# A two-layer decoder on one core: query and key turning split, a new order of work, a router with a narrow moving operand

## What is computed

```python
x = ln(x + L0_attn(x))            # 32 heads, low-rank queries and keys, rope, causal
x = ln(x + L0_xattn(ctx_512, x))  # adjacency: top 30% of q.k, mixed with x
x = ln(x + L0_ffn(x))             # 7 experts, 2 chosen per token, and a shared one
x = ln(x + L1_attn(x))            # 16 heads of 16 features, rope, causal
x = ln(x + L1_xattn(x, ctx_512))  # softmax over a normalised bilinear form
x = ln(x + L1_ffn(x))             # silu(x.Wg) * (x.Wu), then Wd; hidden size 1024
```

```python
q = rms_norm(x @ q_a_w, q_a_ln_w) @ q_b_w      # 192 low-rank features, 32 x (128 + 64)
ckv = x @ kv_a_w                               # 64 shared latent features, 64 rotated
k_rot = apply_rope(ckv[..., 64:])
gate = xt @ Wr + br                            # the router: 256 features to 7 experts
_, ids = jax.lax.top_k(gate + gate_bias, 2)
```

## Time and profile before

| | us |
|---|---|
| median of three runs | 673.74 (673.16 to 674.34) |
| profiled execution, own time | 674.2 |
| its span in the trace | 672.3 |
| TensorE busy | 651.7 (97%) |
| VectorE busy | 524.2 (78%) |
| ScalarE busy | 502.5 (75%) |
| GpSimd busy | 389.5 (58%) |
| TensorE's granted clock over the span | 0.997 |

### The profile page before, as it was taken

One profiled execution on the slowest core, in us unless ns is written; L12 is line 12 of the kernel. 1 busy time (PEld: TensorE's weight loads), 2 busy tenths in 40 slices (PEclk: granted clock), 3 DMA queues, 4 the chain that ended last, 5 costly groups with the idle time before them and its releaser, 6 DMA issues.

```text
span 672.3 us, 15731 instructions
## 1 busy us (share of the span) xinstructions
PE 651.7 (97%) x5342; PEld 557.9 (83%) x5342; DVE 524.2 (78%) x1684; ACT 502.5 (75%) x1305; POOL 389.5 (58%) x646
## 2 busy tenths in 40 slices
PE   8899999999999999999999999999989999999996
PEld 5589988989888899889877888889878887778885
DVE  2799988996999799767889945557798878858455
ACT  4799778878688885898887866665658786876544
POOL 3388658457664845698769455545872321445543
PEclk9999999999999999999999999999999999999998
DMA  8763022214213211310032012111020000011201
GB/s 259 188 186 86 18 71 59 77 26 118 49 56 103 49 50 47 95 33 2 1 96 63 1 54 87 48 49 47 1 95 5 3 3 4 3 48 48 94 1 63
DMA packets 35048, 40.17 MB, mean 60 GB/s; under 512 B 7052, under 2 KB 27798, under 8 KB 34968
## 3 DMA queue, kind: packets, MB, share of 16 engines
q1 hardware_dynamic: 34424, 38.84, 19.8%
q10 hardware_dynamic: 544, 0.33, 0.2%
HBM read 29.05 MB, written 1.05 MB: 45 GB/s over the span
## 4 chain that ended last, share of the span: by engine, by line
PE 82%; DVE 7%; ACT 4%; SPq 2%; issue 2%; DMA 1%; POOL 1%; DVEq 0%; POOLq 0%; ACTq 0%
PE bank L1242 72%; PE bank L1256 8%; SPq L2762 1%; PE bank L1542 1%; ACT probs L1922 1%; DMA xT_plain<-in_xT 1%; POOL qT L2487 1%; DVE bn L2034 1%; DMA qT<-xT_plain 1%; DVE ctx_pair_lo L2011 1%; DVE y L2011 1%; DVE probs L2162 1%; DVE g_pair_lo L2011 0%; ACT x L1684 0%; ACT xT_hi L1677 0%
## 5 line engine op out<-in xcount | busy, mean ns | idle before, releaser
L2484 POOL TENSOR_SCALAR probs<-probs,soft 128x256 f32<-128x256 f32 (+1 forms) x256 | 104.9, 432 | 52.1 <-DVE soft L2170 51.0
L1784 ACT ACTIVATE probs<-probs,soft 128x256 f32<-128x256 f32 (+1 forms) x256 | 113.2, 448 | 12.0 <-DVE soft L2162 11.1
L2487 POOL TENSOR_TENSOR w_split_lo<-w_raw,w_split_hi 128x512 fp32r<-128x512 f32 (+2 forms) x57 | 74.3, 1311 | 67.9 <-ACT w_split_hi L1677 67.7
L1242 PE MATMUL bank<-xT_hi,w_split_hi 128*128 128x512 f32 x256 | 103.8, 405 | 3.7 <-DVE xT_lo L2014 2.5
L1242 PE MATMUL bank<-xT_lo,w_split_hi 128*128 128x512 f32 x256 | 100.5, 393 | 0.0
L1242 PE MATMUL bank<-keyT,qT 128*64 128x192 f32 (+3 forms) x1024 | 80.4, 302 | 1.3 <-POOL qT L2487 1.3
L1242 PEld LDWEIGHTS bank<-keyT,qT 128*64 128x64 f32 x1024 | 74.2, 137 | 8.9 <-issue 3.6
L1242 PE MATMUL bank<-xT_hi,w_split_lo 128*128 128x512 f32 x192 | 75.5, 393 | 0.0
L2487 POOL TENSOR_TENSOR qT<-qT,xT_plain 64x512 f32<-64x512 f32 x44 | 56.5, 1283 | 31.8 <-DMA qT<-xT_plain 29.7
L2162 DVE CUSTOM_DVE_ANT_0 probs<-bank,mask 128x128 f32<-128x128 f32 (+1 forms) x192 | 58.0, 330 | 17.2 <-PE bank L1242 16.2
L1677 ACT ACTIVATE probsT<-bank 128x384 f32<-128x384 f32 x128 | 53.6, 494 | 13.9 <-PE bank L1256 13.4
(11 more groups left out here) (259 smaller groups left out, 1820.6 us busy)
## 6 DMA issues: line engine op xcount, KB each, us to landing
qT<-xT_plain SPq DMA_DIRECT2D x88, 64.0 KB, 2.0
w_raw_heads<-in_w_o SPq DMA_DIRECT2D x8, 512.0 KB, 4.6
w_raw<-in_w_nopeT SPq DMA_DIRECT2D x8, 384.0 KB, 3.1
qT<-rope_buf SPq DMA_DIRECT2D x40, 64.0 KB, 2.0
w_raw<-in_w_gateT SPq DMA_DIRECT2D x8, 256.0 KB, 2.7
w_raw<-in_w_upT SPq DMA_DIRECT2D x8, 256.0 KB, 3.1
w_raw<-in_w_downT SPq DMA_DIRECT2D x8, 256.0 KB, 3.6
w_raw<-in_L_ffn_Wup SPq DMA_DIRECT2D x7, 256.0 KB, 2.6
```

Source lines behind the costliest of these rows:

```text
L1242: return t.matmul(out, lhsT, rhs, start=start, stop=stop, skip_group_check=shared)
L1784: ins = s.activation(p[:, at], p[:, at], ACT.Exp, bias=st[:, 0, r:r + 1], scale=-1.0, accum_out=st[:, 1, r:r + 1])
L2484: return g_.tensor_scalar(out, in0, s1, s2, op0, op1)
L2487: return g_.tensor_tensor(out, in0, in1, op)
```

## The change

The edits, beside the names and lines that follow from them.

1. **Keys apart.** `down_T h` keeps the eight query blocks; the four key blocks become `key_T h`, with its own signal `keyT_copied`. On VectorE the keys' scaling is its own step `key_scale`.
2. **Early root table.** ScalarE runs a dummy Sqrt (into `last_root`) behind its two load issues at the start.
3. **First loads.** `xT0`, `xT1`, then the weights of groups 0 and 1, then `xT2`.
4. **Two early query buffers.** `q 0 0 0` needs `down_T 0` alone, `q 0 0 1` also `key_T 0`; the first gets a buffer of its own (`qT_first`), both have fixed places.
5. **Router.** The tokens (`xT_hi`, `xT_lo`, 128x128) are stationary and 14 columns move: the seven of `w_router` as fp32r and the seven of its rest (`w_router_parts`, made by two VectorE instructions in the constants' step). Sixteen matmuls a half as before, each now on the whole array; the copy and the transposition are gone, VectorE adds the two parts.
6. **The end.** `f_end` is cut: `f_mid 0` (batch 2, blocks 4 to 6), `f_mid 2` (batch 3, tile 1, blocks 4 to 6), `f_end 0` (batch 2, block 7), `f_mid 1` (tile 0, blocks 4 to 6), `f_end 1` (both tiles, block 7).
7. **Last store** of eight is issued by ScalarE's queue. In `out1` the bias matmuls of both tiles come first.
8. **Order.** A new `PE_ORDER` (523 steps), a new `ASIDE`, new costs, and a cost of leaving each grouping of the array (`LEAVE`) in place of one `MODE`.

```diff
 PE_ORDER = steps_of("""
-down 0, w_k 0, down 1, w_q 0, down_T 0, w_v 1, w_k 1, q 0 0 0, down_T 1, w_q 1, adj_w, w_v 0, adj_qk, q 0 0 1,
-q 1 0 0, s 0 0 0, s 1 0 0, q 1 0 1, adj_sim 0, s 0 0 1, ...
+down 0, down 1, down_T 0, w_k 0, key_T 0, w_q 0, adj_w, w_k 1, w_v 0, w_v 1, key_T 1, down_T 1, adj_qk, q 0 0 0,
+q 0 0 1, adj_sim 0, q 1 0 0, w_q 1, w_k 2, s 0 0 0, q 1 0 1, s 1 0 0, s 0 0 1, ...
...
-f_up 1 7, f_end 0, f_end 1""")
+f_up 1 7, f_mid 0, f_mid 2, f_end 0, f_mid 1, f_end 1""")
...
-    ("adj_mask", 2, 1): 193, ("att_mix", 3): -60, ("down_root", 1): -24, ...
+    ("adj_mask", 2, 1): 58, ("adj_top", 1, 8): 146, ("down_root", 1): 5, ...
...
-    HOP, TABLE, MODE = 0.2, 1.3, 0.13
+    HOP, TABLE = 0.2, 1.3
+    LEAVE = {"": 0.09, "cols64": 0.13, "cols32": 0.135, "rows64": 0.085, "quarter": 0.13}
...
-LOADS_AFTER = [("xT0", "xT1"), ("xT1", "xT2")] + [("xT2", name) for name in (
+LOADS_AFTER = [("xT0", "xT1"), ("xT1", 0), ("xT1", "xT2")] + [("xT2", name) for name in (
...
-FIRST_Q = ("q", 0, 0, 0)
+EVERY_TURNED = [(name, h) for h in range(NHALF) for name in ("down_T", "key_T")]
+TURNED_FOR = {("q", 0, 0, 0): [("down_T", 0)], ("q", 0, 0, 1): [("down_T", 0), ("key_T", 0)]}
+MID_TILES = [[(0, j) for j in range(TB)], *[[(1, j)] for j in range(TB)]]
+LAST_STORED = (B - 1, TB - 1)
+EARLY_PLACE = {("q", 0, 0, 0): (0,), ("q", 0, 0, 1): (1,)}
...
+            elif name == "key_T":
+                h, = k
+                w.wait_ge(*landed("identity"))
                 w.wait_ge(*key_rot[h])
                 out = wait_bank(("keyT", h))
                 for i, tile in enumerate(tiles_of[h]):
                     w.wait_ge(*key_lat[tile])
                     ins = transpose(out[:, i * P:(i + 1) * P], key_tok[:, tile, :])
-                ins.then_inc(lowT_ready.sem, 1)
+                ins.then_inc(keyT_ready.sem, 1)
...
             elif name == "route_lin":
...
-                terms = [(c, plain(part)) for c in range(DC) for part in (xT_pair.hi, xT_pair.lo)]
-                for n, (c, xt) in enumerate(terms):
-                    for i, tile in enumerate(tiles_of[h]):
-                        ins = mm(out[32 * i:32 * i + NE, 0:P], w_router[:, c, :], xt[:, c, tile * P:(tile + 1) * P],
-                                 n == 0, n == len(terms) - 1, True)
+                terms = [(part, c) for c in range(DC) for part in (xT_pair.hi, xT_pair.lo)]
+                for i, tile in enumerate(tiles_of[h]):
+                    for n, (part, c) in enumerate(terms):
+                        ins = mm(out[:, i * 2 * NE:(i + 1) * 2 * NE], part[:, c, tile * P:(tile + 1) * P],
+                                 w_router_parts[:, c, :, :], i == 0 and n == 0, n == len(terms) - 1, True)
                 ins.then_inc(route_ready.sem, 1)
-            elif name == "route_gate":
-                h, = k
-                w.wait_ge(*route_copied[h,])
-                transpose(wait_bank(step)[:, 0:P], gate_T[h][:, :]).then_inc(route_ready.sem, 1)
...
                 for i in range(TB):
+                    mm(out[:, i * D:(i + 1) * D], ones1[:, :], bias1[:, 3 * D:], i == 0, False, True)
+                for i in range(TB):
                     part = out[:, i * D:(i + 1) * D]
-                    mm(part, ones1[:, :], bias1[:, 3 * D:], i == 0, False, True)
...
+                    w.wait_ge(*zeroed["unit"])
+                    s.activation(last_root[:, 0:1], plain(ones1[:, 0:1]), ACT.Sqrt)
...
+        b, i = LAST_STORED
+        w.wait_ge(*last_normed[b, i])
+        s.dma_start(out_dram[b, i * P:(i + 1) * P, :], x[:, TB * b + i, :]).then_inc(stored[b], 16)
...
+                    own(v.tensor_copy(w_router_parts[:, :, 0, :], w_router[:, :, :]))
                     w.wait_ge(*own.now)
+                    own(tt(w_router_parts[:, :, 1, :], w_router[:, :, :], plain(w_router_parts[:, :, 0, :]), ALU.subtract))
```

253 lines of the change are left out of this document (134 added, 119 removed), and 4 rows, old and new, of the table ASIDE.

## The result

| | before | after |
|---|---|---|
| time, median of 11 executions, same chip | 674.22 us (673.16 to 675.29) | 678.15 us (675.67 to 681.76) |
| profiled execution, span | 674.2, 672.3 | 678.62, 676.7 |
| mean granted clock | 0.997 in the profiled execution; 0.992 to 0.999 in the executions of the comparisons below | 0.984 to 0.996 in the 11 |

The ratio is 1.0053, with a 95% interval of 1.0036 to 1.0071. The change makes the kernel slower by some 4 us; the prediction was 672.3, in a range of 669.0 to 675.3. Within the 11 executions of after the time goes with the clock: 675.67 at 0.996, 678.15 at 0.991, 681.76 at 0.984.

A forecast was written before the change was run, and what follows sets the result against it. TensorE, busy 651.7 of 672.3 us, was taken as the bound. The terms -1.5 + 1.3 - 0.1 + 0.4 - 1.4 = -1.3 gave 672.9 for an execution like the profiled one; forecast median 672.3, range 669.0 to 675.3.

The forecast's parts named there:

- start, to the first scores: From the start to the first scores: -1.5 us, from -1.85 + 0.3; ends -2.7 and -0.3.
- switches: TensorE's switches between array groupings: 13 more at 0.10 each, +1.3 us; ends +0.8 and +1.7.
- router's own work: Router on TensorE: 32 matmuls at 0.085, 2.7 us against 2.8 before, -0.1; ends +0.6 and -1.9.
- waits in the middle: TensorE's waits between start and end: half of the 2.8 us left would go, -1.4; ends -2.8 and +2.
- end: After the cut of `f_end`: VectorE starts 0.6 later, last store gives -0.25; +0.4 us, ends 0 and +0.7.
- the 2.50 wait is filled: Start, before `q 0 0 0`: `adj_w` and six other steps placed ahead fill TensorE's 2.50 us wait for turned queries.
- first scores after 38: Start: a sign that the prediction would be wrong, if the first scores came after 38 us.
- The chain is 1.28 shorter: Start: the root table's load leaves half 0's chain, 1.28 us shorter, `xT_lo` near 20.3 rather than 23.09.
- Rival E: Router: the load's duration sets the pace, +0.6 rather than -0.1, 673.0 us; part of the forecast's range, no separate chance.
- D: Attention: `pv` waits for `probsT` in 8 places where `pT` and `pv` stand close; +4, about 676.5 us; chance 0.18.
- B: Start gives nothing: `xT2` lands near 14 rather than 12.5, the 1.5 go; 673.7 to 674 us; chance 0.22.
- no wait over 0.5 before `q 0 0 0`: Start: sign expected in the profile after, TensorE waiting nowhere over 0.5 us before the first query step.

The follow-up runs named there:

- run 12: Also before_root_only: kernel before, with one early dummy square root on ScalarE so that its table loads at the start; 674.73 us, ratio 0.9996.
- before_router_early: Kernel before, with the second half's old router directly behind TensorE's wait for the turned tokens; 674.0 us, ratio 0.9992.
- run 8: Also after_warm_wait: changed kernel, with twelve unread products of 512 columns in `adj_w` before its wait; 675.82 us, ratio 1.0028.
- run 5: Kernel before, with the new router's narrow products directly behind the wait for the turned tokens; 677.44 us, ratio 1.0046.
- Run 6: Changed kernel, with the router's 16 columns moved eight times over (128 moving columns); 678.98 us, ratio 1.0074.
- runs 1 and 3: Changed kernel. 1: second half's router behind the first expert's first pass, 683.66 us; 3: also `adj_w` behind the weights' steps of groups 0 and 1, 685.09 us.
- after_ww_rows_later: Changed kernel, with 128-column router, twelve products in `adj_w`'s wait and GpSimd's clearing of second-layer rows behind `e_u 4 1`; 675.27 us, ratio 1.0004.
- after_tuned: Changed kernel, with 128-column router, `adj_w` later, group 2's loads behind the first queries' swap, `w_k 2` behind the first scores, other engines replanned; 683.0 us.
- after_wide_and_warm: Changed kernel, with 128-column router and twelve products in `adj_w`'s wait, GpSimd's clearing not moved; 677.74 us, ratio 1.0031.
- runs 13 and 6: 13: changed kernel, twelve products in `adj_w`'s wait, second half's router moved behind `e_u 0 1` on TensorE alone, 679.15 us; 6: see Run 6.
- run 7: The run after_ww_rows_later: changed kernel, 128-column router, `adj_w`'s wait filled, GpSimd's clearing moved behind `e_u 4 1`; 675.27 us, ratio 1.0004.

## Why the prediction was wrong

Time by term, from the profiled executions:

| term | forecast | measured |
|---|---|---|
| start, to the first scores | -1.5 | +1.0, with 1.7 of clock in it |
| switches | +1.3 | 9 x 0.1 fit the +1.0 of the first attention; not measured one by one |
| router's own work | -0.1 | +0.75 |
| clock behind the router | not foreseen | +3.4 |
| waits in the middle | -1.4 | idle time: -0.15 in the first attention, -0.2 in the experts, -0.76 in the second layer |
| end | +0.4 | +0.6 |

**The start: the step that failed** is "the 2.50 wait is filled". I listed `adj_w` among the steps that fill it and did not ask what `adj_w` itself waits for: I worked out SP's queue for `xT2` and not for this load, issued at 17.45. That is 2.93 us where the term had none, with some 1.7 of clock behind it. The prediction's own sign of being wrong, first scores after 38, is what came (39.13). What I had looked at came out: 1.50 for `xT2` (I said 1.2), `xT2`'s issue at 7.16 (6.6). "The chain is 1.28 shorter" was wrong by itself too, as run 12 shows: the table was not on the chain alone. `xT_lo` did come early, at 18.67, more than that term allows; the table alone gives none of it. In after's trace the three weight splits stand behind `xT_lo` and the first half's keys are scaled by 15.7, so VectorE's order is what differs; no run here tried that alone.

**The clock: a mechanism that was on no list.** I read in the earlier trace rows a granted clock of 1.00 in all stretches and took it for a constant. In the profiled execution of before it was one. It isn't in each: in before_root_only and before_router_early, with the same start, it fell behind the wait of 2.5 us. The change puts the router's narrow products behind a wait, where the clock fell each time, and a longer wait in the start, where it fell in two of three profiled executions; neither my terms nor my rivals priced this. The runs say how much: filling the start's wait gives back 2.3 us (run 8), the narrow form alone costs 3.4 (run 5), of which 0.75 is its pace (both against runs of other comparisons). These do not add up to the 3.9 of the medians, as the clock differs from execution to execution, and each run carries other small waits.

**The router: the right mechanism, the wrong end of it.** I put its pace between 0.028 and 0.107 and chose 0.085, by the turnings of the earlier trace rows. It was 0.111: 32 x 0.111 = 3.55 against 2.8 before, +0.75. The 0.83 ns a column from the earlier trace rows, which I made the upper end, was the pace. The Trainium skill, "TensorE: Matmul & The Clock Gate", section on LDWEIGHTS, has a load of P columns take P/1.2 ns, 107 ns for 128 by estimate, and the pace in the trace agrees within 4 ns. Run 6 shows the same pace for 16 and for 128 moving columns. Rival E had it right. In the experts' +3.07, 3.4 of clock and 0.75 make 4.15; waits are 0.2 less, and some 0.9 that remain I cannot place.

**Switches and waits in the middle.** Nine switches more by 0.10 are +0.9, and the first attention lost 0.96 while TensorE's idle time went from 2.03 to 1.88. So the switch term fits, and the wait term did not hold for this part: the 1.01 at 227.56 is gone, and this has come,

```profile
120.16 0.65 PE L1251 MATMUL bank<-keyT,qT_first 128*64 128x192 f32 x4 [1.08 <-POOL qT_first L2509]
```

a wait for the same kind of operand. In the second layer idle time went from 4.27 to 3.51, -0.76, of which `kT`, 0.78 before and 0.23 now, is the largest part. The other 0.45 of the -1.2 is less busy time, where four switches more should have added 0.4; I cannot place it. In sum the waits gave 1.1 of my 1.4, near in size by luck: most of it lay in places that I had counted as fixed.

**The end** measured +0.56 for +0.4: batch 2's addition comes 4.22 us behind `f_end`'s start, before 3.53, so 0.69 for my 0.6, and what follows it, the last store among it, gave back 0.13 of my 0.25.

```profile
668.05 0.69 DVE L2028 TENSOR_TENSOR y<-bank,x 128x512 f32<-128x512 f32 x1 [1.88 <-PE bank L1251]
```

**The rivals.** D, the slower one, had the sign and not the mechanism: TensorE waits nowhere for `probsT`. B's `xT2` landed at 11.8 and not at 14. The signs that I had named would have told: no wait over 0.5 before `q 0 0 0` (it is 2.93), first scores at 36 to 37 (39.13). The chance of slower, 0.18, came from one mechanism alone; that another of the list's moved steps might find its transfer late had no share in it.

## What to carry to other kernels

When a step is moved forward to fill a wait, look up the last transfer it needs and when that is issued; the wait is filled only by steps whose inputs are there. Ask of every stretch with a wait what stands behind it: here products with 16 moving columns behind a wait of 1.08 us cost 3.4 us in clock, more than the wait itself, and with 128 columns behind it they cost no clock. Work put into the wait of the start kept the clock there. And in a kernel whose orders are planned from one another, move a single engine's row with the rest frozen before a time is put down to the move: runs 1 and 3 moved VectorE's program as well, which nobody had meant to change, and so could not say what the move itself cost.

## What the runs showed of the hardware that I had not expected

- The granted clock fell to half for stretches that cost 1.7 or 3.4 us each where TensorE was at work throughout. With 16 moving columns behind the wait it fell each time: 1.08, 1.13, 1.16 and 1.38 us. Behind 1.04 to 1.38 us for the same operand with 128 or more columns it did not, in fourteen executions. It also fell behind the router's first half, with a wait of only 0.2 ahead, in one of the seven profiled executions that have the narrow form there (after_warm_wait), and at 493 behind one of 0.80 (after_ww_rows_later).
- Waits of 1.5 us and more went both ways, whatever stood behind: for `xT2` 1.50, 1.91 and 2.03 without a fall, 1.87 and 2.41 with one; for `adj_w` 2.01 without, 2.18 and 2.93 with; for `u_pair_lo`, with 512 columns behind, 2.66 in after_tuned and 2.67 in after_wide_and_warm without, 2.54 and 2.66 in runs 13 and 6 with; the 2.50 of before without, and in before_root_only and before_router_early with one. What decides between those no run here can tell, and one kernel's executions differ in it.
- A product with 128 stationary columns and a new load each time starts every 0.111 us whether 16 or 128 columns move; the four turnings of the earlier trace rows at 0.085 are faster, and no run here tells why.
- One small conversion on VectorE took 0.17 to 0.19, 1.0 to 1.24, or 3.63 us. That the 3.63 was GpSimd's clearing, run 7 shows; the 1.23 there ends with an instruction of GpSimd, which no run took away.
